# Bias product over 128 rows, relative tags on GpSimd, node loads of x on the sync engine

## What is computed

```python
h = relu(layernorm(x))
msg_input = concat([h[src], h[dst]], axis=1)
for t in range(4):
    m = relu(msg_input @ W1[t] + b1[t]) @ W2[t] + b2[t]
    msgs += where(edge_type == t, m, 0)
agg = segment_sum(msgs, dst)                 # one row for each node
gi = agg @ W_ih.T + b_ih ; gh = h @ W_hh.T + b_hh
r, z = sigmoid(i_r + h_r), sigmoid(i_z + h_z)
n = tanh(i_n + r * h_n)
out = x + (1 - z) * n + z * h
```

## Time and profile before

| | |
|---|---|
| median of 3 runs | 1900.25 us (1898.24 to 1906.78) |
| profiled execution | 1895.2 us, its span 1893.3 us |
| mean granted TensorE clock | 0.972 of full speed |
| PE busy / PEld busy | 1688.8 us (89%) / 1422.2 us (75%) |
| DVE busy | 1791.1 us (95%) |
| ACT busy | 1539.3 us (81%) |
| POOL busy | 1130.8 us (60%) |
| DMA, mean | 169 GB/s, 319.52 MB |

### The profile page before, as it was taken

One profiled execution on the slowest core, in us unless ns is written; L12 is line 12 of the kernel. 1 busy time (PEld: TensorE's weight loads), 2 busy tenths in 40 slices (PEclk: granted clock), 3 DMA queues, 4 the chain that ended last, 5 costly groups with the idle time before them and its releaser, 6 DMA issues. The chain is left out here.

```text
span 1893.3 us, 44349 instructions
## 1 busy us (share of the span) xinstructions
PE 1688.8 (89%) x10156; PEld 1422.2 (75%) x10156; DVE 1791.1 (95%) x4457; ACT 1539.3 (81%) x3793; POOL 1130.8 (60%) x1788
## 2 busy tenths in 40 slices
PE   0112599999999999999999999999999999999898
PEld 0002488888888888888888888888888888888787
DVE  8999989999999999999999999999999999999887
ACT  0011499999998899999999999999999999998796
POOL 5654677777777565655556565555656556565310
PEclk9995599999999999999999999999999999999999
DMA  2112467777776766777776777777777776779853
GB/s 67 42 34 53 109 178 192 195 193 191 192 190 180 193 185 187 194 189 188 191 190 185 192 191 188 189 193 186 189 194 191 186 195 187 187 192 169 165 140 97
DMA packets 477058, 319.52 MB, mean 169 GB/s; under 512 B 106707, under 2 KB 463139, under 8 KB 476966
## 3 DMA queue, kind: packets, MB, share of 16 engines
q10 hardware_dynamic: 261792, 156.12, 27.5%
q1 hardware_dynamic: 185734, 106.93, 24.2%
q0 software_dynamic: 29440, 55.47, 13.0%
HBM read 211.59 MB, written 106.72 MB: 168 GB/s over the span
## 5 line engine op out<-in xcount | busy, mean ns | idle before, releaser
L570 POOL DMA_INDIRECT e_x<-in_x,rows_now x816 | 795.6, 975 | 277.1 <-issue 271.0
L1127 ACT ACTIVATE e_h<-e_x,shift,rstd 128x128 f32<-128x128 f32 x816 | 356.6, 491 | 116.0 <-DVE shift L993 116.0
L1144 ACT ACTIVATE n_h<-n_x,shift,rstd 128x128 f32<-128x128 f32 x784 | 361.2, 487 | 0.0
L1288 PE MATMUL bank<-n_h_hi,whh_hi 128*128 128x512 f32 x588 | 248.8, 423 | 8.4 <-ACT n_zc L1244 7.9
L1288 PE MATMUL bank<-n_a_hi,wih_hi 128*128 128x512 f32 x588 | 248.8, 423 | 0.0
L1016 DVE TENSOR_SCALAR n_sel<-iota,n_rel 128x256 fp32r<-128x256 f32 x784 | 240.0, 368 | 4.8 <-ACT n_rel L1195 4.8
L1364 PE MATMUL bank<-n_sel,n_win 128*128 128x256 f32 x1568 | 236.0, 293 | 5.8 <-DVE n_sel L1016 5.8
L1290 PE MATMUL bank<-n_a_hi,wih_lo 128*128 128x512 f32 x588 | 232.7, 396 | 0.0
L1289 PE MATMUL bank<-n_h_lo,whh_hi 128*128 128x512 f32 x588 | 232.5, 395 | 0.0
L1290 PE MATMUL bank<-n_h_hi,whh_lo 128*128 128x512 f32 x588 | 231.8, 394 | 0.0
L1289 PE MATMUL bank<-n_a_lo,wih_hi 128*128 128x512 f32 x588 | 231.8, 394 | 0.0
(11 more groups left out here) (170 smaller groups left out, 4208.6 us busy)
## 6 DMA issues: line engine op xcount, KB each, us to landing
n_win<-messages SPq DMA_DIRECT2D x1568, 64.2 KB
messages<-e_msg ACTq DMA_DIRECT2D x204, 257.0 KB, 2.7
n_x<-in_x ACTq DMA_DIRECT2D x195, 256.0 KB
out<-n_out ACTq DMA_DIRECT2D x195, 256.0 KB
e_x<-in_x,rows_now POOLq DMA_INDIRECT x816
rows_now<-lists SPq DMA_DIRECT2D x204, 2.0 KB
lists<-picks,list_rows POOLq DMA_INDIRECT x72
w<-in_W SPq DMA_DIRECT2D x1, 512.0 KB
```

Of the source, the lines that this page charges most:

```text
L570: G.indirect_dma_start(e_x[:, s, 2 * end + t, :], None, x, bass.IndirectOffsetOnAxis(ap=rows_now[:, s, t, end:end + 1], axis=0)).then_inc( ...
L1127: last = A.activation(e_h[:, s % 2, k, :], e_x[:, s, k, :], ACT.Relu, scale=rstd[:, slot, col + k:col + k + 1], bias=shift[:, slot, col + ...
L1144: last = A.activation(n_h[:, s % 2, cols], n_x[:, s, cols], ACT.Relu, scale=rstd[:, slot, col + 4 + k:col + 5 + k], bias=shift[:, slot, co ...
L1288: T.matmul(o, w_hi, v_hi, start=start, stop=False)
```

## The change

Three edits. `b2_rows` and `row_is` grow from 2 to 128 partitions, with b2 in high and low parts in the first two rows and zeros below, and the bias product runs over all 128 rows. The two ACTIVATE for `n_rel` go from ACT, and one `tensor_tensor` on POOL does the same, between the two gathers of the source end and the two of the destination end. `load_x` goes from ACT to SP, where it stands between `load_rows` and the windows. Its wait is the same.

```diff
--- before.py
+++ after.py
@@ -124,8 +124,8 @@
         bsum = sb("bsum", [P, 3])
         bneg = sb("bneg", [P, 3])
         b1_cols = sb("b1_cols", [P, TYPES])
-        b2_rows = sb("b2_rows", [2, TYPES * D], F32R)
-        row_is = sb("row_is", [2, 2])
+        b2_rows = sb("b2_rows", [P, TYPES * D], F32R)
+        row_is = sb("row_is", [P, 2])
 
 
         records = sb("records", [P, ECOLS, 2], I32)
@@ -221,7 +221,7 @@
         in_column = borrow(n_zc[:], ECOLS, ECOLS)
 
         b2_two, b2_hi, b2_lo, b2_parts = (
-            e_msg[:].rearrange("p r t w -> p (r t w)")[0:2, at * TYPES * D:(at + 1) * TYPES * D] for at in range(4))
+            e_msg[:].rearrange("p r t w -> p (r t w)")[:, at * TYPES * D:(at + 1) * TYPES * D] for at in range(4))
         b2_two, b2_parts = b2_two.bitcast(F32), b2_parts.bitcast(F32)
 
         ends = n_d[:].rearrange("p r w -> p (r w)").bitcast(I32).rearrange("p (k e c) -> p k e c", k=SEGMENTS, e=2)
@@ -436,7 +436,7 @@
             sp.dma_start(bih[:], b_ih).then_inc(s_weights, 16)
             sp.dma_start(bhh[:], b_hh).then_inc(s_weights, 16)
             sp.dma_start(b1_cols[:], b1.rearrange("t p -> p t"), allow_slow_non_contiguous=True).then_inc(s_weights, 16)
-            sp.dma_start(b2_two[:], b2.rearrange("(a t) o -> a (t o)", a=1).to_broadcast([2, TYPES * D])
+            sp.dma_start(b2_two[:], b2.rearrange("(a t) o -> a (t o)", a=1).to_broadcast([P, TYPES * D])
                          ).then_inc(s_weights, 16)
             sp.dma_start(last_i, dst_cols[P - 1:P, :].to_broadcast([P, ECOLS])).then_inc(s_last, 16)
 
@@ -482,6 +482,21 @@
                         sp.wait_ge(g_starts, 1)
                     sp.wait_ge(s_starts, 16)
 
+            def load_x(i, m):
+                g, s = i - LAG + 9, (m - LAG + 9) % UNROLL
+                if not within(g, NG):
+                    return
+                if due(g - 7):
+                    sp.wait_ge(n_xhed, g - 7)
+                if isinstance(g, int) and g == NG - 1:
+                    for k, rows in parts:
+                        sp.dma_start(n_x[0:rows, s, k * D:(k + 1) * D],
+                                     x[g * GROUP + k * P:g * GROUP + k * P + rows, :]).then_inc(n_loaded[s], 16)
+                else:
+                    sp.dma_start(n_x[:, s, :].rearrange("p (k d) -> p k d", k=TILES),
+                                 x[bass.ds(g * GROUP, GROUP), :].rearrange("(k p) d -> p k d", p=P)
+                                 ).then_inc(n_loaded[s], 16)
+
             def step(i, m):
                 q, s = i + 2, (m + 2) % UNROLL
                 if within(q, UNITS):
@@ -491,6 +506,7 @@
                         if due(q - 7):
                             sp.wait_ge(e_tagged, q - 7)
                     load_rows(q, m + 2)
+                load_x(i, m)
                 if isinstance(i, int) and i == HEAD - 1:
                     for k in range(segment_of(q) + 1, SEGMENTS):
                         for pair_ in range(2):
@@ -563,9 +579,9 @@
                 if side:
                     pool.wait_ge(l_left[job % 2], (job // 2 + 1) * len(PIECES) * 16)
 
-            def gather(q, m):
+            def gather(q, m, ends_):
                 s = m % UNROLL
-                for end in range(2):
+                for end in ends_:
                     for t in range(2):
                         G.indirect_dma_start(e_x[:, s, 2 * end + t, :], None, x,
                                              bass.IndirectOffsetOnAxis(ap=rows_now[:, s, t, end:end + 1], axis=0)
@@ -609,6 +625,19 @@
                 transfers_may_start(h + 1)
                 write_half(h)
 
+            def relative_tags(g, m):
+                s = m % 4
+                if not within(g, NG):
+                    return
+                if isinstance(g, int) and g == 0:
+                    pool.wait_ge(s_bases, 1)
+                pool.wait_ge(n_windowed[s], uses(g, s, 4, 128))
+                if due(g - 1):
+                    pool.wait_ge(n_seled, g - 1)
+                G.tensor_tensor(n_rel[:, s % 2, :].rearrange("p (h k) -> p h k", h=2),
+                                n_win[:, s, :, TAG].bitcast(F32).rearrange("p (h k) -> p h k", h=2),
+                                base[:, bass.ds(2 * g, 2)].unsqueeze(2).to_broadcast([P, 2, 2]), ALU.add).then_inc(n_reled, 1)
+
             def inverse_roots(i, m):
                 first = i - 5
                 if m % 4 != 1 or not within(first, LN_END):
@@ -650,7 +679,10 @@
                     wait_half(h)
                 transfers_may_start(i + 1 + 2 * TYPES)
                 if within(i, UNITS):
-                    gather(i, m)
+                    gather(i, m, (0,))
+                relative_tags(i - LAG + 1, m - LAG + 1)
+                if within(i, UNITS):
+                    gather(i, m, (1,))
                 if h is not None:
                     write_half(h)
                 inverse_roots(i, m)
@@ -802,8 +834,8 @@
                 dve.wait_ge(s_split, N_SPLITS)
                 V.tensor_tensor(whh_lo[:], whh[:], whh_hi[:].bitcast(F32), ALU.subtract)
                 V.tensor_tensor(wih_lo[:], wih[:], wih_hi[:].bitcast(F32), ALU.subtract)
-                V.tensor_scalar(row_is[:, 0:1], part[0:2, :], 0.5, None, ALU.is_lt)
-                V.tensor_scalar(row_is[:, 1:2], part[0:2, :], 0.5, None, ALU.is_gt)
+                V.tensor_scalar(row_is[:, 0:1], part[:], 0.0, None, ALU.is_equal)
+                V.tensor_scalar(row_is[:, 1:2], part[:], 1.0, None, ALU.is_equal)
                 link(V.tensor_tensor(b2_lo[:], b2_two[:], b2_hi[:].bitcast(F32), ALU.subtract))
                 link(V.tensor_scalar(b2_parts[:], b2_hi[:].bitcast(F32), row_is[:, 0:1], None, ALU.mult))
                 V.scalar_tensor_tensor(out=b2_rows[:], in0=b2_lo[:].bitcast(F32), scalar=row_is[:, 1:2],
@@ -1147,21 +1179,6 @@
                 if 3 in tiles:
                     last.then_inc(n_normed, 1)
 
-            def load_x(i, m):
-                g, s = i - LAG + 9, (m - LAG + 9) % UNROLL
-                if not within(g, NG):
-                    return
-                if due(g - 7):
-                    act.wait_ge(n_xhed, g - 7)
-                if isinstance(g, int) and g == NG - 1:
-                    for k, rows in parts:
-                        act.dma_start(n_x[0:rows, s, k * D:(k + 1) * D],
-                                      x[g * GROUP + k * P:g * GROUP + k * P + rows, :]).then_inc(n_loaded[s], 16)
-                else:
-                    act.dma_start(n_x[:, s, :].rearrange("p (k d) -> p k d", k=TILES),
-                                  x[bass.ds(g * GROUP, GROUP), :].rearrange("(k p) d -> p k d", p=P)
-                                  ).then_inc(n_loaded[s], 16)
-
             def store_messages(i, m):
                 q, s = i - 10, (m - 10) % UNROLL
                 if within(q, UNITS):
@@ -1183,18 +1200,6 @@
                                   n_out[:, s, :].rearrange("p (k d) -> p k d", k=TILES)).then_inc(n_stored[s], 16)
 
             def step(i, m):
-                g, s = i - LAG + 1, (m - LAG + 1) % 4
-                if within(g, NG):
-                    if isinstance(g, int) and g == 0:
-                        act.wait_ge(s_bases, 1)
-                    act.wait_ge(n_windowed[s], uses(g, s, 4, 128))
-                    if due(g - 1):
-                        act.wait_ge(n_seled, g - 1)
-                    for half in range(2):
-                        rows = slice(2 * half, 2 * half + 2)
-                        last = A.activation(n_rel[:, s % 2, rows], n_win[:, s, rows, TAG].bitcast(F32), ACT.Identity,
-                                            bias=base[:, bass.ds(2 * g + half, 1)])
-                    last.then_inc(n_reled, 1)
                 normalise_edges(i, m, (0, 1, 2))
                 g, s = i - LAG, (m - LAG) % 2
                 if within(g, NG):
@@ -1220,7 +1225,6 @@
                     A.activation(n_a_hi[:, s, :], bank[BA][:], ACT.Copy).then_inc(n_ahi, 1)
                 normalise_nodes(i, m, (0,))
                 store_out(i, m)
-                load_x(i, m)
                 q, s = i - 9, (m - 9) % 2
                 if within(q, UNITS):
                     act.wait_ge(e_hid, q + 1)
@@ -1315,7 +1319,7 @@
                             last = T.matmul(bank[1][:, cols], w1[:, t, 1, :], g_ht[:, D:2 * D], start=False, stop=True)
                         last.then_inc(g_hid, 1)
                         pe.wait_ge(g_relued, c + 1)
-                        T.matmul(bank[2][:], ones_r[0:2, :], b2_rows[:], start=True, stop=False)
+                        T.matmul(bank[2][:], ones_r[:], b2_rows[:], start=True, stop=False)
                         for t in range(TYPES):
                             last = T.matmul(bank[2][:, t * D:(t + 1) * D], g_r[:, t, :], w2[:, t, :],
                                             start=False, stop=t == TYPES - 1)
@@ -1386,7 +1390,7 @@
                 if within(q, UNITS):
                     pe.wait_ge(e_relued, q + 1)
```

(2 more changed lines are left out.)

## The result

The changed kernel takes 2653.66 us in the median (2649.27 to 2659.76), the kernel before 1902.68 us in the runs beside it. The ratio is 1.395, with a 95% interval of 1.392 to 1.399. The direction was foreseen and the time lies in the stated range, but 164 us above the 2490 us.

A forecast was written before the change was run, and what follows sets the result against it. PE was taken to set the pace at 8.35 us a step; after the change, a ring of 11.55 us over 188 steps (2171.4 us), plus 239.9 before, 71.1 behind and small allowances, gave 2490 us, range 2370 to 2750.

The forecast's parts named there:

- the ring: `n_xh`, load_x on SP, windows, tags, `n_sel` and `n_xh` of the next step, each awaiting the one before: 11.55 us.
- the landing: From the last window's issue until its data has arrived: 2.1 us, between 1.4 and 2.7, making 2360 to 2605 us.
- rival C: 256 KB of x ahead of the windows in SP's queue delays them 1.35 us: 12.9 us a step, 2740 us; chance 0.10.
- the two wake-ups: Waking another engine on either side of the tags on POOL: up to 0.1 us each, within the 0.4 us allowed.
- Rival D: PE's clock falls while it stands; if not hidden, the ring has 13.3 us, 2815 us in all; chance 0.06.
- Rival B: Windows on SP are not late; the step falls to PE's and DVE's need, 8.08 us: 1845 us; chance 0.07.
- edit 1: Bias product on PE over 128 rows instead of two: 0.28 us less each, 57 us over 204 units if PE sets the pace.

The follow-up runs named there:

- the last experiment: The changed kernel with 15 matmuls of 512 columns added in each loop step where TensorE waits for the selection matrices: 2704.00 us.

## Why the prediction was right, and where it was off

**The mechanism** was right at each step: load_x waits for the `n_xh` of its own step, the windows stand behind it, and `n_sel` of the next step behind those. A wait one count lower, or windows ahead of it, removes the loss, and shortening the ring by 0.77 us removes 143 us. That the time lies in the stated range is in part luck: 2654 us is above the 2605 that the landing alone could reach, and the range went up to 2750 to take in rival C, which is not what happened. One bound was added up wrongly, too: the upper bounds of the terms sum to 13.1 us a step and some 2780 us, not to 13.4 and 2840.

**The sum** was 11.55 us and the mean turn 12.46. The terms, as means of 187 turns of the changed kernel's trace, with mine in brackets: wake-up 0.16 (0.1), issue of load_x 0.37 (0.40), to the first window 1.07 (0.85), windows 4.69 (4.64), last window's issue to the start of the tags 2.81 (2.1 and half of the two wake-ups), tags to `n_sel` 0.24 (the rest of 0.4), DVE 3.12 (3.06). The term that was mis-sized is the landing: with the tags behind it 3.05 us where I had 2.5, which is 0.55 of the 0.91 us. The page's median for windows is 2.3 us, near the 2.1 that I took between two far rows, but it is the last window that counts, and it flies together with the message store, with gathers, or with both in over half of the turns. My estimate from the Trainium skill (DMA: Bandwidth & Descriptors, Anatomy of one DMA), 2.15 us for one transfer on GpSimd's path, is just under that median; the fit has no term for other transfers in flight. The second term, 0.22 us, was the way to the first window, with SP's register load in it, for which I used 0.53 us of the earlier trace rows; in the changed kernel its median is 0.83:

```profile
L518 SPq TENSOR_LOAD <-starts_row x196: 520/826/1217, 219.6 to 2621.1; - x196
```

It is slower there because 104 of the 188 turns, and not 46, are of the sort with a store 0.6 to 1.4 us ahead (the table of the last experiment), as far as sorting can tell. The longest of the earlier trace rows, 1.19 us, had hinted at that sort.

**Rival C** named the right term for the wrong reason: the landing was longer, but x in front of the windows cost 0.05 us a step. **Rival D**: the clock did fall, to a mean of 0.885, and PE's time at it was hidden as forecast. That keeping it up would cost 50 us I had not seen. **Rival B** rested on the rule of the Trainium skill (DMA: Bandwidth & Descriptors, Issuing engines are not separate DMA queues) that the place of issue matters only for the sequencer. With the wait met early, the two variants on SP agree with it: 1895 and 1891 us. The rule is silent on a wait that goes with the issue, and that was the 760 us.

**The price of B, and of edit 1,** was wrong. I had PE as the only bound, since it was busy without a gap, and gave the wide product 55 us. Its 0.28 us are real. But ACT's order, with the load's issue in it, was as long as TensorE's. The sign was in the waits of the kernel before, between 500 and 1700 us, and I passed over it as room:

```profile
ACT e_r L1232 <- issue: 53.4, 143, 1.2
```

This is 0.37 us a step in which ACT stands while its sequencer issues the load of x. With all three edits and the ring open the time was 1891 us, and 1872 with the tags left on ACT, not 1845.

**POOL** fitted in its step as forecast: it stood 1042.5 us for windows. But in the open ring the tags on it cost some 19 us, for which rival B had put down nothing.

## What to carry to other kernels

A wait that moves to another engine must be priced by what is queued behind it there, and by how far that engine ran ahead: here 0.4 us of issuing came with 4 us a step. Look for the ring that the wait closes, add up its terms by rows, and test it by changing the order in it, or the count waited for by one, before blaming queues or bytes. Where a busy engine has no gap, ask whether a second one is bound to the same length; then each edit alone pays little and both together pay: here 5, 14 and 31 us.

## What the runs showed of the hardware

- A higher TensorE clock made the kernel slower, 2704 against 2654 us: it moved a 257 KB store into company with the last windows, and a 256 KB store to about 1 us ahead of a register load on SP. The time from the last window's issue to its use was 2.34 us with neither store nor gather near, 2.88 us with one of them (the gather alone in 5 steps only) and 3.60 us with both.
- 192 KB less in the same queue straight ahead of eight windows of 64 KB changed the step by 0.05 us. What was in flight at the end of the windows mattered, what went ahead of them didn't.
- A bias product over 2 rows costs 0.28 us more in the stream of 128-row matmuls than one over 128 rows. This agrees with the Trainium skill, TensorEngine Tiling (Array Packing), Key Properties, that a change of tiling mode drains the engine, though no run shows the drain itself.
- A load of eight words from on-chip memory into SP's registers took 0.52 to 0.64 us in the changed kernel, but 0.81 to 1.22 us wherever ACT had issued a 256 KB store 0.6 to 1.4 us before it. Two more kernels sort the same way in the mean; that the store is the cause wasn't tried.
